# A cross-attention and mixture-of-experts kernel on one core: row turns of x, context and the router's rows moved from TensorE to transposing DMAs

## The reference

```python
x = x + xattn(layernorm(x), ctx, ctx, mask)      # x, ctx: (16, 256, 256); 16 heads of 16
x = x + ffn(layernorm(x))
# xattn: q = Q Wq + b, k = K Wk + b, v = V Wv + b; softmax(where(mask == 0, -1e9, q k^T / 4)) v; Wo
# ffn: top 2 of 8 experts by softmax(h gate^T), silu(h g^T) * (h u^T) through expert_down (352 wide),
#      weighted by the scores, plus sigmoid(h s^T) * a shared expert of width 704
```

## Time and profile before

| | |
|---|---|
| median of 3 runs | 852.09 us (846.51 to 854.3) |
| profiled execution | 849.35 us, of which the span from first to last instruction is 847.1 us |
| granted TensorE clock, mean | 0.966 of 2.4 GHz |
| busy | PE 755.6, DVE 546.0, ACT 397.2, POOL 335.4 us |

### The profile page before, as it was taken

One profiled execution on the slowest core, in us unless ns is written; L12 is line 12 of the kernel. 1 busy time (PEld: TensorE's weight loads), 2 busy tenths in 40 slices (PEclk: granted clock), 3 DMA queues, 4 the chain that ended last, 5 costly groups with the idle time before them and its releaser, 6 DMA issues.

```text
span 847.1 us, 21926 instructions
## 1 busy us (share of the span) xinstructions
PE 755.6 (89%) x8123; PEld 465.7 (55%) x8123; DVE 546.0 (64%) x1174; ACT 397.2 (47%) x679; POOL 335.4 (40%) x499
## 2 busy tenths in 40 slices
PE   4778999978889898987989879999999999979987
PEld 3444555544545555553455646677777777634644
DVE  6766788877878888776665687433333333356677
ACT  4235566455555556564555453444444444322231
POOL 6222345564764544453313240112212122475660
PEclk9889999989999999998999999999999999987999
DMA  5654555645554444545420223788988897642742
GB/s 175 170 154 138 174 170 176 187 124 137 156 162 129 149 114 132 159 130 153 117 62 30 82 88 94 140 167 163 166 175 170 160 158 159 146 124 75 228 120 69
DMA packets 164234, 118.26 MB, mean 140 GB/s; under 512 B 108450, under 2 KB 143522, under 8 KB 164132
## 3 DMA queue, kind: packets, MB, share of 16 engines
q1 hardware_dynamic: 146564, 82.44, 40.7%
q0 software_dynamic: 9552, 26.10, 10.1%
q10 hardware_dynamic: 8016, 8.33, 3.0%
HBM read 52.78 MB, written 38.14 MB: 107 GB/s over the span
## 4 chain that ended last, share of the span: by engine, by line
PE 58%; DVE 18%; issue 7%; ACT 7%; DMA 3%; another core or an unknown queue 2%; SPq 2%; ACTq 1%; POOL 1%; DVEq 0%; POOLq 0%
PE ps_st L1887 14%; PE ps_st L1459 10%; PE ps_m L1902 8%; DVE mx L994 7%; PE ps_st L1099 5%; PE ps_o L1150 4%; PE ps_m L1173 3%; PE ps_o L1470 3%; PE ps_m L1470 2%; PE ps_m L1249 2%; PE ps_st L1118 2%; ACT p L803 2%; PE ps_st L1134 1%; PE ps_st L1470 1%
## 5 line engine op out<-in xcount | busy, mean ns | idle before, releaser
L994 DVE TENSOR_REDUCE mx<-ps_st 128x4 f32<-128x1024 f32 x128 | 155.7, 1218 | 54.6 <-PE ps_st L1118 27.8
L803 ACT ACTIVATE p<-ps_st 128x1024 f32<-128x1024 f32 x128 | 131.0, 1023 | 86.1 <-PE ps_st L1134 68.1
L1887 PE MATMUL ps_st<-fwh,p 128*128 x568 | 137.9, 313 | 1.7 <-DMA p<-expert_rows 1.7
L1660 POOL DMA_DIRECT2D sorted_out<-p x71 | 38.4, 541 | 181.2 <-ACT p L1717 177.5
L1887 PE MATMUL ps_st<-fwl,p 128*128 x284 | 88.7, 312 | 0.0
L1391 POOL DMA_INDIRECT expert_rows<-hrow,slot x64 | 64.3, 1005 | 48.6 <-DVE slot L1382 27.5
L1099 PE MATMUL ps_st<-maskq,identb 64*64 64x512 bf16 x512 | 53.6, 408 | 30.0 <-DVE mx L994 27.4
L1459 PE MATMUL ps_st<-q,arena 128*128 128x512 f16 x264 | 67.0, 407 | 6.3 <-issue 6.0
L1887 PEld LDWEIGHTS ps_st<-fwh,p 128*128 128x128 f16 x568 | 55.6, 98 | 28.6 <-issue 2.1
L1099 PE MATMUL ps_st<-mb_k,identb 64*64 64x512 bf16 x256 | 52.7, 408 | 16.6 <-ACT p L803 13.6
L1668 POOL DMA_INDIRECT p<-sorted_out,xn x52 | 53.6, 1031 | 26.9 <-issue 14.5
(11 more groups left out here) (237 smaller groups left out, 1747.7 us busy)
## 6 DMA issues: line engine op xcount, KB each, us to landing
arena<-ffn_dram SPq DMA_DIRECT2D x20, 544.0 KB
sorted_out<-p POOLq DMA_DIRECT2D x71, 128.0 KB, 2.9
qk_scratch<-arena SPq DMA_DIRECT2D x32, 256.0 KB
qk<-qk_scratch SPq DMA_DIRECT2D x44, 128.0 KB, 3.0
arena<-ctx_dram SPq DMA_DIRECT2D x16, 256.0 KB
hT_dram<-hT ACTq DMA_DIRECT2D x16, 256.0 KB, 2.4
out_dram<-xr SPq DMA_DIRECT2D x16, 256.0 KB
xr<-x_dram SPq DMA_DIRECT2D x7, 512.0 KB, 4.2
```

Of the source, the lines that this page charges most:

```text
L803: eng.activation(expo[n % 4][:, :, :], ps_st[pair["T", n]][:, :].rearrange("p (h q) -> p h q", h=4), ACT.Exp, scale=SCALE).then_inc(s_e, 1)
L994: eng.tensor_reduce(mx[b % 2][:, qt, :].rearrange("p (h g j) -> p h g j", h=2, g=HG)[:, :, hg, :], ps_st[pair["S", 8 * b + n]][:, :].rearr ...
L1887: last = mm(o[:, 0:INTER], xgT[k % NXG][:, xl, dc, :], (fwh, fwl)[wl][:, bass.ds(e, 1), w0 + dc * INTER:w0 + (dc + 1) * INTER], start=dc = ...
```

## The change

For batches 3 to 15 x and context no longer go through PE. ACT copies the rows as high half (`xh` at 8b - 2, `ch` at 8b - 1) and DVE subtracts for the low half (`xl` at 8b - 1, `cl` at 8b), both into new row buffers `rows`, and SP issues one transposing DMA for each of the two, of 128x1024 fp16. For batches 0 to 12 `hrow` is turned the same way from SP. Batches 0 to 2 (x, context) and 13 to 15 (`hrow`) stay as they were. `nrm` moves from 8b - 2 to 8b - 3, the store of `hT` from unit 7 to unit 2 of the next iteration, `slots_of` behind unit 1's maximum for iterations 7 to 15, and the first two parts of `route` three units forward. The order of the halves in `xT`, `cT`, `hT` changes with it; readers index accordingly.

```diff
+        TURNED = NB - 3
+        for b in range(TURNED):
+            del when["ht", b]
+            when["tw", b] = 8 * (b + 6) + 2
...
+        for b in range(BY_PE, NB):
+            del when["xt", b], when["ct", b]
+            when.update({("nrm", b): 8 * b - 3, ("xh", b): 8 * b - 2, ("xl", b): 8 * b - 1,
+                         ("ch", b): 8 * b - 1, ("cl", b): 8 * b})
+        for b in range(NB - 3):
+            when["pick", b] = when["route", b] - 3
...
             def load_c(b):
-                if b:
+                if b > BY_PE:
+                    eng.wait_ge(s_cl, b)
+                elif b:
                     eng.wait_ge(s_ct, b)
...
             for i in range(ITER):
+                if BY_PE <= i < NB:
+                    eng.wait_ge(s_xl, i + 1)
+                    eng.wait_ge(s_q, i)
+                    eng.dma_start_transpose(turned_rows[0], xrow[:, :, :, :].rearrange("p a l d -> p (a l d)")).then_inc(s_xd, 16)
                 b = i - 2
                 if 0 <= b < NB:
                     eng.wait_ge(s_nm, b + 1)
                     eng.dma_start(m_scratch[b, :, :], nm[:, :]).then_inc(s_mw, 16)
+                if BY_PE <= i < NB:
+                    eng.wait_ge(s_cl, i + 1)
+                    eng.wait_ge(s_k, i)
+                    eng.wait_ge(s_v, i)
+                    eng.dma_start_transpose(turned_rows[1], crow[:, :, :, :].rearrange("p a l d -> p (a l d)")).then_inc(s_cd, 16)
...
+                b = i - 5
+                if 0 <= b < TURNED:
+                    eng.wait_ge(s_rh, b + 1)
+                    eng.wait_ge(s_rl, b + 1)
+                    if b:
+                        eng.wait_ge(s_rt, b)
+                        eng.wait_ge(s_tw, 16 * b)
+                    eng.dma_start_transpose(hT[:, :, :, :, :].rearrange("p a l c t -> p (a l c) t"),
+                                            hrow[b % 3][:, :, :].rearrange("p a w -> p (a w)")).then_inc(s_thd, 16)
                 if 3 <= i < NB:
                     join(eng, i - 3)
...
                     for b in now("tw", i, u):
+                        if b < TURNED:
+                            eng.wait_ge(s_thd, 16 * (b + 1))
...
+                    for b in now("xl", i, u):
+                        eng.wait_ge(s_xh, b + 1)
+                        eng.tensor_tensor(xrow[:, :, 1, :], xn[:, :, :], xrow[:, :, 0, :], ALU.subtract).then_inc(s_xl, 1)
+                    for b in now("cl", i, u):
+                        eng.wait_ge(s_ch, b + 1)
+                        eng.tensor_tensor(crow[:, :, 1, :], c32[:, :, :], crow[:, :, 0, :], ALU.subtract).then_inc(s_cl, 1)
+                    if u == 1 and 7 <= i < NB:
+                        slots_of(eng, link, moe, i - 7)
...
+                    for b in now("pick", i, u):
+                        routing = route(eng, link, moe, b, s_sel)
+                        next(routing)
+                        next(routing)
...
                         elif kind == "rt":
                             wait_bank(eng, (kind, b))
-                            eng.wait_ge(s_th, b + 1)
+                            if b < TURNED:
+                                eng.wait_ge(s_thd, 16 * (b + 1))
...
                         elif kind == "q":
+                                eng.wait_ge(s_xd, 16 * (b - BY_PE + 1))
                         elif kind == "k":
+                                eng.wait_ge(s_cd, 16 * (b - BY_PE + 1))
```

## The result

The changed kernel takes 861.09 us (median of 4 runs, 857.52 to 863.54), the kernel before in the same set 849.3 (839.19 to 854.3): ratio 1.021, 95% interval 1.012 to 1.031. The forecast was 851, no change; it is slower by more than the noise, though whether by more or less than 2% the interval leaves open. The time lies inside the stated range (832 to 870), in the part that had a chance of 0.27. The profiled execution took 861.56 us, 12.2 more than that of before.

What follows compares the result with a forecast made beforehand. It took PE to bound early iterations and PE and DVE to share the bound from about iteration 6. Terms of -2.8, -1.4, +0.9, +2 and +1 summed to -0.3 us, so 851 us, no change, range 832 to 870.

Steps and rivals of the forecast that it cites:

- the part that had a chance of 0.27: Whole kernel: the outcome of being slower than the kernel before by over 1%.
- What leaves PE: PE in attention: 26.5 us removed, worth 1.4 us each in iterations 3 and 4, 0.7 in 5 and 6, 0.3 later.
- first rival: PE throughout the attention: it bounds, so up to all 26.5 us come back; taken at 838 us, chance 0.30.
- What is moved on DVE: DVE's path from iteration 7 on: +0.35 in unit 7, +0.35 in unit 2, -0.3 in unit 5; +0.1 net with `ct`.
- Turns by DMA, x: SP's turn of x, issued in unit 7: lands at 313.4, hidden by 4 us before `q` in unit 3.
- Context: SP's turn of the context: lands near 317, hidden by 3 us before `k` in unit 4, at longest landing 1.5.
- `hrow`: SP's turn before the router in unit 0: lands at 309.0, no slack; cost 0, bounds 0 and +1 per iteration.
- second rival: Router in unit 0, PE's queue: `hrow`'s turn lands late, up to 866 us at the row's maximum; chance 0.20.
- Behind `hrow`'s turn: SP's later loads delay POOL's list: ACT's wait grows, +2 us in iteration 7, +1 in iteration 9.
- The clock: PE's clock: less PE work brings three more drops of 3 to 4 us, +11, giving 862 us; chance 0.08.
- The sum: Whole kernel: all terms together -0.3 us on the profiled execution's 849.35, giving 849.1.
- The forecast's own sign of being wrong: Late iterations shrinking by over 1 us, or PE standing at L1416, L1173 or L1309 for the turns.

Runs made afterwards that it cites:

- after_plain: Changed kernel without the scatter (rows stored in their own order by plain DMAs from ACT's queue, routing left out): ratio 1.016 to the kernel before.
- before_plain: Kernel before without the scatter (rows stored in their own order by plain DMAs from ACT's queue, routing left out): ratio 0.999 to the kernel before.
- x_first: Changed kernel with both DVE moves undone and the x turn issued ahead of x's load and the second half of weights: ratio 1.048 to the kernel before.
- fillers: Changed kernel with PE turning constants nobody reads where the removed turns stood, giving PE its old load back: ratio 1.023 to the kernel before.
- turns_only: Changed kernel with both DVE moves (slots_of, route) undone, all three turns still by DMA: ratio 1.029 to the kernel before.
- order_only: Changed kernel with all turns back on PE, only DVE's order of slots_of and route changed: ratio 1.009 to the kernel before.
- pick_only: Kernel before with only the first two parts of route three units earlier: ratio 1.014 to the kernel before, 1.011 when run again as pick_only_c.

## Why the prediction was wrong, point by point

- *What leaves PE.* The count was right (24 matmuls are left at L1225 and 24 at L1479). Its worth was still too high: iterations 3, 4 and 5 took 22.6, 22.6 and 22.1 us between the maxima of unit 0, against 22.1, 23.2 and 22.8, in sum -0.8 where I had -3.5, and DVE's wait for PE in 82 to 105 rose from 6.3 to 8.1 instead of falling to 3.5. That it is worth next to nothing late was right: 25.0 against 24.9. The first rival (PE bounds throughout) is refuted by this.
- *What is moved on DVE.* Forecast +0.1 an iteration, measured +0.1 in the changed kernel where the clock held, +0.4 in after_plain against before_plain. Term by term there: unit 7 +0.32 for `xl` (forecast 0.35); unit 2 +0.27 (0.35). Unit 5 was to lose, by at most 0.3, and gained 0.66; units 4 and 6 gave 0.43 and 0.51 back, where only the context's 0.3 had been counted. So two places were read rightly, one had the wrong sign, and that the sum is near is in part luck.
- *Turns by DMA, x.* **This is the step that failed.** "Hidden by 4 us" rested on a landing of 4.8 us and an issue right behind the join, both read in iteration 12. But behind the join come x's load and, from iteration 5 to 9, the second half of weights, which I had counted as work behind `hrow`'s turn and not as work ahead of the x turn of the next iteration. It was issued at 132.3, landed in 9.9 us and cost 6.3 us of PE and 7.4 of the span. PE was ready for `q` at 136.05: with a landing of 4.8 us the late issue alone would have cost 1.1 us, the long landing made the other 5.1. x_first shows the place in the queue as a cause (3.7 us in iteration 6 against 9.6), and that changing places only moves the wait to POOL's list. It isn't the only one, as fillers shows (5.5 us from the same place). What differs there is ACT's load of `rb`, which ran beside the turn in the changed kernel and behind it in fillers; after_plain and turns_only, where it ran beside the turn's end, have 7.0 and 9.6 us. No run moves this load alone, so its share is not shown.
- *Context.* One wait of 1.1 us, in iteration 7, where the forecast had none; nearly right. *`hrow`* landed 1.6 us sooner than taken, no wait: the second rival is refuted. *Behind `hrow`'s turn.* This term was wrong for the changed kernel: the ACT wait for POOL in iteration 7 fell from 3.5 to 2.0 us where I had +2 (iteration 7 took 28.7 us, 28.8 before). With `hrow` alone turned by DMA the wait is there, 4.7 us against 2.4 in order_only; that the long stand in iteration 6 hides it in the changed kernel is likely but not shown. Iteration 9 grew by 2.4 where I had +1, but not by a wait of ACT for POOL, of which it has none; a fall of the clock stands in it.
- *The clock.* The rival with chance 0.08 is in the result: falls at 233.9, 271.4, 322.6, 373.8 and 404.6 us. A late iteration with one is 1.1 to 1.2 us longer than one without here, not 3 to 4 (the iteration of the earlier trace rows with 28.7 us had waits of its own), in order_only 1.6. Its reason was wrong: PE's smaller load is not what brings them, since fillers has as many. What does is not shown. In order_only a late completion stands before the fall, but fillers has the same completion without a fall, and on the faster chips, where no completion is late, the clock falls five times between 100 and 440 us in after_plain and once in before_plain. Which of the two DVE moves brings the falls on the slower chips stays open.
- *The sum.* Forecast -0.3, measured +12.2. Against its terms: x turn +7.4 (0), late iterations +3.9, nearly all by the clock (+0.1 an iteration), early ones -0.8 (-3.5), iteration 7 -0.1 (+2), iteration 9 +2.4 (+1), iteration 8 -2.7 (0); the rest is ahead of iteration 1 and behind the attention. The forecast's own sign of being wrong, PE standing for a turn at the projection of `q`, came true.

## What to carry to other kernels

Before a transfer is called hidden, write down everything issued ahead of it on its queue back to the last idle time, in the iteration where most else is loaded, and take its landing from there; a median landing says nothing of that iteration. Then look at what the other queues load at that moment. Work taken off an engine is worth what the chain between its neighbours gives back: here DVE's unit-by-unit path, read as distances between successive maxima, told within 0.3 us an iteration what 26 us less of PE were worth, though not in every unit. And where a step is moved, ask what it now runs beside on POOL, and price it with the steps that move with it, not alone. An equal total is no proof of an equal kernel: fillers and the changed kernel have the same ratio, and their iterations differ by 2 to 5 us in both directions.

## What the runs showed of the hardware

- In the sets where before took 849 to 856 us, PE's completions came 1.5 to 4.2 us after the last matmul's start (0.3 in most blocks) while POOL issued its indirect DMAs, wherever these stood; in the sets with 813 us never. DVE's idle for "remote" before its maxima from 100 to 400 us was 19.7 us in before, and none in any profile of the faster kind. This isn't the whole difference between the chips: after the last maximum before needs 442 us, the kernels of the faster kind 419 to 430, and what makes this stretch longer was not looked into.
- A DVE instruction beside POOL's subtraction takes longer. Two rows of pick_only_c, which fall into POOL's low half, against the same operations of before_plain, which start just as it ends (DVE, then POOL in each):
```profile
326.63 0.66 DVE L923 TENSOR_TENSOR rsa<-rstd,anyq 128x2 f32<-128x2 f32 x1
327.33 1.08 DVE L931 TENSOR_SCALAR xn<-xr,mv,rsa 128x256 f32<-128x256 f32 x2
...
325.26 2.68 POOL L674 TENSOR_TENSOR fwl<-arena,fwh 128x272 f16<-128x272 f32 x4
```
```profile
289.09 0.25 DVE L883 TENSOR_TENSOR rsa<-rstd,anyq 128x2 f32<-128x2 f32 x1
289.38 0.73 DVE L889 TENSOR_SCALAR xn<-xr,mv,rsa 128x256 f32<-128x256 f32 x2
...
286.64 2.69 POOL L640 TENSOR_TENSOR fwl<-arena,fwh 128x272 f16<-128x272 f32 x4
```
That is 0.8 of the 0.9 us that pick_only loses in unit 6. The Trainium skill (Advanced Engine Details and Errata, GPSIMD Details) says that POOL shares a read and a write interface with DVE and conflicts with DVE instructions that run in a two-port mode or have two inputs in SBUF. `rsa` has two, and the rows agree. `xn` has one input tensor; whether it ran in such a mode no run here shows, and it is slower beside POOL as well.
- The same page of the Trainium skill (X-Bar Transpose (TRN2)) says that transposing DMAs are as fast as regular ones. Per byte they are not here: queue q1 had 82.44 MB in 40.7% of 16 engines' span before and 92.67 MB in 47.7% after, so the 39 turns took about 1040 engine-us for 10.2 MB, 102 per MB, against 67 per MB for the queue before. The trace's packets say why: a turn is 1024 packets of 256 bytes, 27.7 ns each in the attention, and the queue's plain packets of 512 bytes take 28.8. Per packet the two cost about the same; a turn has more of them per byte.
```profile
q1 hardware_dynamic: 187748, 92.67, 47.7%
```
